# A decoder layer with a top-2 expert stage: gate and residual row move from the last stage into the expert stage

## The chip, the cores and the metric

One core of a Trainium2 chip (trn2) runs the whole layer in one launch. The metric is the device time of that launch in microseconds: the median of three runs. Beside it stands one profiled execution, from which all rows are taken. Names used below: TensorE is PE in the profile, VectorE is DVE, ScalarE is ACT, GpSimd is POOL and SyncE is SP.

## What is computed

Input `x` is 32 sequences of 128 rows of 128 numbers. A first block (an attention block with a scan and a feed-forward part), a cross attention over a context, and an expert layer follow each other, each with a residual and a layer norm. Only the last third matters here:

```python
logits = jnp.einsum('bsh,eh->bse', x, Wr)              # 8 experts
probs = jax.nn.softmax(logits, axis=-1)
top_v, top_i = jax.lax.top_k(probs, 2)
top_v = top_v / jnp.sum(top_v, axis=-1, keepdims=True)  # the two gates
for e in range(8):
    w_e = jnp.sum(jnp.where(top_i == e, top_v, 0.0), axis=-1)
    h = gelu(jnp.einsum('bsh,mh->bsm', x, W1[e]) + b1[e])   # 128 -> 512
    y = jnp.einsum('bsm,hm->bsh', h, W2[e]) + b2[e]         # 512 -> 128
    out = out + y * w_e[..., None]
x = layernorm(x + out)
```

## The kernel before

All is float32. It has a setup, a loop over 8 groups of 4 sequences (tiles of 128 rows), a routing table, an expert stage and a last stage. Five engines run programs of their own, written out by hand, and meet at semaphores; each engine works through its program in order.

**Group loop.** For each group the layer's first two blocks are computed, the router picks two experts per row, and both copies of the row are written to `expert_in` in DRAM by GpSimd (`rows_out`: 8 indirect DMAs, one per sequence and choice). What is written is `xb_rows[k]`, 132 columns wide: 128 of the row and 4 more, of which the first is the row's "home", its place in `expert_out`. VectorE writes the home (L1238) and the normalised row `xb` (`ln_apply`, L1240). ScalarE copies `xb` to the second tile (L652), GpSimd copies it back into `x_all` (L838) for the residual of the last stage. The two gates go to `gate_all` (L1280 to L1283). Later on VectorE computes the slots (`slot_u`, L1302), after which GpSimd may scatter.

**Expert stage.** The rows now lie in `expert_in` ordered by expert, padded to tiles of 128. There are 72 tiles (`TILES`). A table `tab` in SBUF holds each tile's expert and first row; engines read it with `value_load`. For tile j:

- SyncE: `row_in` loads the 128 rows into `xt` (four buffers) once TensorE has turned the tile four before (`turned`); `home_of` loads the four further columns into `home` (eight buffers).
- TensorE: `turn_rows(j+2)`, `hidden(j+1)` (L1773), `outputs(j)` (L1782). `outputs` waits for `y_added` of two tiles before, since it reuses the bank.
- VectorE: `turned_rows(j+2)` copies the turned tile out of its bank (L1349, `xnT`), `weights(j+2)` copies the expert's first matrix (L1355), `results(j)` adds the bias `b2` to the output and writes `ysb` (L1363, `xa`).
- ScalarE: `gelu(j)` (L669).
- GpSimd: `results_out(j)` scatters `ysb` to `expert_out` at the homes (L850).

The tile names are those of the memory that is reused: `xn` is `xt`, `xnT` is `xtT`, `xa` is `ysb`, `qT` is `w1c`, `hT` is `hx`, `mix` is `two_rows`.

**Last stage.** Eight groups again. SyncE loads the two expert results of each row (`rows_back`, L519, 512 KB for a group, four groups in flight). ScalarE multiplies the first by its gate (`first_part`, L685, four instructions), GpSimd adds the residual from `x_all` (`first_sum`, L864), VectorE multiplies the second by its gate and adds (`combine`, L1395, four instructions), then takes statistics (L1401, L1405), GpSimd makes scale and shift of them (`last_scale`, L870 to L880), ScalarE applies them (`last_norm`, L694), SyncE stores (L525). `rows_back(g+4)` is issued behind `store(g)` on SyncE and waits for `combined` of group g.

## Time and profile before

| | us |
|---|---|
| median of 3 runs | 929.15 (928.66 to 929.34) |
| the profiled execution | 929.04 |
| its span, first to last instruction | 927.2 |
| setup and scan, up to the first group's work | about 0 to 100 |
| group loop and routing table, until the first expert tile is loaded | to about 721 |
| expert stage, 72 tiles | about 721 to 881 |
| last stage | 881 to 927.2 |

Busy time over the whole span: TensorE 690.2 us (74%), VectorE 544.1 (59%), ScalarE 373.0 (40%), GpSimd 365.1 (39%). Mean granted clock of TensorE 0.877 of full speed.

How to read the profile: a row gives start, length, engine, line, operation, the tile written and the tiles read, the shape, and in brackets how long the engine had been idle and what ended that. "issue" means that nothing shown in the profile ended the wait: the engine's own sequencer was not there yet. A busy share is an average over stages whose limits differ, so each stage is read by itself.

### The profile page before, as it was taken

How to read it: one execution, taken by the hardware profiler on the slowest of the kernel's cores; microseconds unless marked ns; L12 is line 12 of the kernel's file. 1: busy time of each engine (PE TensorE's matmuls, PEld its weight loads, DVE VectorE, ACT ScalarE, POOL GpSimd, SP SyncE). 2: the span in 40 equal slices, each digit the busy share in tenths (PEclk: the TensorE clock that was granted, in tenths of full speed). 3: DMA queues.
4: the chain of work that ended last, by engine and by line, in shares of the span. 5: the costliest groups of instructions: out<-in, count | busy, mean ns of one | idle time of the engine just before them, and what ended most of it. 6: DMA issues, size and time to landing. Idle time of an engine off the chain costs nothing.

```text
span 927.2 us, 21485 instructions
## 1 busy us (share of the span) xinstructions
PE 690.2 (74%) x6159; PEld 497.4 (54%) x6160; DVE 544.1 (59%) x1733; ACT 373.0 (40%) x790; POOL 365.1 (39%) x514
## 2 busy tenths in 40 slices
PE   4517887896887887886988789788783799999900
PEld 1303645644744753653664564474462799989900
DVE  4585665676666576576576666657656244444443
ACT  2002344353362352443444336235331355555545
POOL 2533260361253145047036026214405255545545
PEclk9557998998997997999899799799797699999955
DMA  8400000000000000000000000000022222222244
GB/s 265 158 12 1 1 31 8 1 20 15 0 12 23 0 12 23 0 12 23 0 0 26 9 0 13 22 0 12 23 90 65 51 63 63 63 61 62 52 150 129
DMA packets 45528, 36.43 MB, mean 39 GB/s; under 512 B 20059, under 2 KB 39452, under 8 KB 45249
## 3 DMA queue, kind: packets, MB, share of 16 engines
q1 hardware_dynamic: 37312, 23.09, 9.0%
q0 software_dynamic: 4608, 9.59, 3.1%
q10 hardware_dynamic: 3584, 3.48, 1.1%
q8 instruction: 9, 0.15, 0.1%
q14 instruction: 15, 0.12, 0.0%
HBM read 23.35 MB, written 12.76 MB: 39 GB/s over the span
## 4 chain that ended last, share of the span: by engine, by line
PE 45%; DVE 19%; issue 11%; another core or an unknown queue 9%; POOL 6%; ACT 3%; DMA 3%; DVEq 1%; SPq 0%; POOLq 0%; ACTq 0%
PE bank L1488 10%; PE bank L1782 8%; PE bank L1773 7%; PE bank L1525 4%; POOL rstd L768 3%; PE bank L1646 3%; DVE stats L1055 3%; PE bank L1573 2%; DVE xn L1064 2%; PE bank L1633 2%; PE bank L1654 2%; PE bank L1615 2%; DVE hT L1104 2%; DVE mv L1060 2%
## 5 line engine op out<-in xcount | busy, mean ns | idle before, releaser
L765 POOL TENSOR_SCALAR vare<-mv 128x1 f32<-128x1 f32 (+1 forms) x112 | 25.9, 231 | 341.1 <-DVE mv L1060 339.5
L850 POOL DMA_INDIRECT expert_out<-xa,home x72 | 80.0, 1111 | 82.6 <-DVE xa L1363 47.7
L669 ACT ACTIVATE hT<-bank,qT 128x128 f32<-128x128 f32 x288 | 81.9, 370 | 64.9 <-PE bank L1773 64.8
L568 ACT ACTIVATE mix<-bank 128x512 f32<-128x512 f32 x128 | 66.1, 602 | 93.8 <-remote 79.0
L1171 DVE TENSOR_REDUCE negmax<-bank 128x4 f32<-128x512 f32 x128 | 79.7, 683 | 18.6 <-remote 10.1
L1782 PE MATMUL bank<-w_t,hT 128*128 x576 | 81.6, 285 | 3.9 <-ACT hT L669 3.9
L799 POOL DMA_INDIRECT expert_in<-xb_rows,slot_u x72 | 71.2, 989 | 25.5 <-issue 19.7
L1773 PE MATMUL bank<-xnT,qT 128*128 128x128 f32 x576 | 80.9, 285 | 0.2
L1104 DVE TENSOR_TENSOR hT<-bank,decay 128x512 f32<-128x512 f32 x72 | 46.4, 686 | 53.6 <-PE bank L1525 53.6
L1488 PE MATMUL bank<-xqT,w_qkv 128*128 128x512 f32 x144 | 71.7, 615 | 5.3 <-DVE x L1160 5.3
L1782 PEld LDWEIGHTS bank<-w_t,hT 128*128 128x128 f32 x576 | 70.8, 194 | 6.3 <-issue 4.9
L1773 PEld LDWEIGHTS bank<-xnT,qT 128*128 128x128 f32 x576 | 72.4, 197 | 3.3 <-issue 2.8
L1488 PE MATMUL bank<-w_qkv,xqT 128*128 128x512 f32 x72 | 52.2, 820 | 29.5 <-ACT mix L568 22.1
L768 POOL TENSOR_TENSOR rstd<-vare,minus_half 128x1 f32<-128x1 f32 (+1 forms) x112 | 67.6, 603 | 9.9 <-POOL vare L765 1.2
L1355 DVE COPY qT<-w_t 128x516 f32 x72 | 31.0, 430 | 43.6 <-issue 39.4
L568 ACT ACTIVATE hebT<-bank 128x512 f32<-128x512 f32 x36 | 21.5, 597 | 86.1 <-PE bank L1573 86.1
L1573 PE MATMUL bank<-hT,v_sb 128*64 128x128 f32 x576 | 39.4, 278 | 15.3 <-DVE x L1160 9.1
L1633 PE MATMUL bank<-qm,kr 32*128 32x128 f32 x512 | 26.8, 335 | 28.5 <-DVE negmax L1171 16.6
L1525 PE MATMUL bank<-qT,kT 64*128 64x128 f32 x576 | 41.8, 285 | 7.3 <-ACT mix L568 5.8
L568 ACT ACTIVATE cT<-bank 128x512 f32<-128x512 f32 x32 | 19.1, 597 | 68.6 <-PE bank L1646 68.6
L1363 DVE TENSOR_TENSOR xa<-bank,b_bc 128x128 f32<-128x128 f32 x72 | 21.0, 292 | 43.7 <-PE bank L1782 29.7
L1633 PEld LDWEIGHTS bank<-qm,kr 32*128 32x128 f32 x512 | 22.4, 235 | 41.7 <-DVE negmax L1171 22.5
(289 smaller groups left out, 1442.9 us busy)
## 6 DMA issues: line engine op xcount, KB each, us to landing
xn<-expert_in SPq DMA_DIRECT2D x72, 64.0 KB
mix<-expert_out SPq DMA_DIRECT2D x8, 512.0 KB, 4.0
ctxT<-in_ctxT SPq DMA_DIRECT2D x9, 256.0 KB, 2.7
w_t<-in_w_t ACTq DMA_DIRECT2D x1, 2064.0 KB, 8.6
xT_all<-in_xT SPq DMA_DIRECT2D x4, 512.0 KB, 5.7
x_all<-in_x SPq DMA_DIRECT2D x4, 512.0 KB, 9.0
w_t<-in_w_t SPq DMA_DIRECT2D x1, 2048.0 KB, 7.4
expert_in<-xb_rows,slot_u POOLq DMA_INDIRECT x72
```

The lines of the kernel that those rows point to most:

```text
L568: nc.scalar.activation(dst, src_ap, func, scale=scale, **kw).then_inc(free[BANK[name]], 1)
L669: ins = nc.scalar.activation(hx[n][:, c, :], bank[2 + n][:, c * P:(c + 1) * P], ACT.Gelu, bias=w1c[n][:, FF + c:FF + c + 1])
L768: nc.gpsimd.tensor_tensor(rstd[stage][:, t:t + n], vare[stage][:, t:t + n], minus_half[:, 0:n], ALU.pow).then_inc(rstd_ready[stage], n)
L799: nc.gpsimd.indirect_dma_start(xs[:, :], bass.IndirectOffsetOnAxis(ap=slot_u[:, t, k:k + 1], axis=0), xb_rows[k][:, t, :], None).then_inc( ...
L850: nc.gpsimd.indirect_dma_start(ys[:, :], bass.IndirectOffsetOnAxis(ap=home[:, n, 0:1].bitcast(U32), axis=0), ysb[n % UNROLL], None).then_i ...
L1104: nc.vector.tensor_tensor(at[t % 2][:, r, :, :], b[:, :].rearrange("p (a n) -> p a n", a=PAIRS), decay[:, t, :].unsqueeze(1).broadcast_to( ...
L1171: nc.vector.tensor_reduce(negmax[t % 2][:, i, 28:28 + XC], b[:, :].rearrange("p (c n) -> p c n", c=XC), AX.X, ALU.max, negate=True).then_i ...
L1488: done(mm(b[:, :], lhsT, rhs, start=True, stop=True), name)
L1525: ins = mm(halves[r][:, tile(p)], kT[rows, p, tile(t)], qT[rows, p, tile(t)], start=True, stop=True)
L1633: ins = mm(b[i][:, tile(c)], kr[rows, c, tile(t)], qm[t % 2][rows, c, :], start=True, stop=True)
L1773: ins = mm(bank[2 + n % 2][:, c * P:(c + 1) * P], w1c[n % 2][:, c * P:(c + 1) * P], xtT[n % 2], start=True, stop=True)
L1782: ins = mm(bank[4 + n % 2][:, 0:P], hx[n % 2][:, c, :], w2_t[:, bass.ds(e, 1), c, :].rearrange("p a n -> p (a n)"), start=(c == 0), stop=( ...
```

## The change

Each scattered row carries what the last stage needed separately. Of the four further columns the first stays the home (`HOME`), the second becomes the row's gate (`GATE`), the third a flag (`OWN`) that is 1 in the copy of the first choice and 0 in the other. VectorE writes the gates straight into `xb_rows`; `gate_all` and GpSimd's copy into `x_all` go. The flag is set once by a memset.

In the expert stage GpSimd multiplies the loaded tile by its flag (`own_rows`, two tiles ahead, into `own`, four buffers), and VectorE's `results` gets a second instruction that multiplies by the gate and adds `own`, after a wait for the first. `y_drained` now tells TensorE that the bank is free; `y_added` comes after the second instruction. SyncE's `row_in` waits also for `own_ready`. VectorE's loop spans eight tiles instead of four.

In the last stage `first_part` and `first_sum` go; VectorE adds the two halves of a group in one instruction. Homes are numbered by partition first, so that the rows of a group that belong to one partition lie together in `expert_out` (4 KB a partition instead of four pieces of 1 KB).

```diff
+HOME, GATE, OWN = P, P + 1, P + 2
...
-        gate_all = sb("gate_all", [P, SEQS, TOPK])
...
-        part = [xf, xab]
+        own = [xab[:, n, :] for n in range(UNROLL)]
...
 # SyncE
             def row_in(j, n, row):
                 sp.wait_ge(turned, j + 1)
+                sp.wait_ge(own_ready, j + 1)
...
-            both = ys[0:SEQS * P * TOPK, :].rearrange("(s p k) n -> p s (k n)", p=P, k=TOPK)
+            both = ys[0:SEQS * P * TOPK, :].rearrange("(p s k) n -> p s (k n)", p=P, k=TOPK)
...
             def rows_back(g, n):
-                sp.wait_ge(combined, g * T + T)
+                sp.wait_ge(combined, g + 1)
...
 # ScalarE: first_part and its calls removed
-                for t in range(T):
-                    ins = nc.scalar.activation(part[n][:, t, :], two_rows[m][:, t, 0, :], ACT.Copy,
-                                               scale=gate_all[:, bass.ds(g * T + t, 1), 0])
...
 # GpSimd
+            nc.gpsimd.memset(xb_rows[0][:, :, OWN:OWN + 1], 1.0).then_inc(pool_const, 1)
...
-                nc.gpsimd.tensor_copy(x_all[:, bass.ds(g * T, T), :], xb[:, :, :]).then_inc(xkept, 1)
...
+            def own_rows(n, xs_in, homes_in):
+                pool.wait_ge(x_in[n % UNROLL], xs_in)
+                pool.wait_ge(home_in[n], homes_in)
+                nc.gpsimd.tensor_scalar(own[n % UNROLL], xt[n % UNROLL], home[:, n, OWN - P:OWN - P + 1], None,
+                                        ALU.mult).then_inc(own_ready, 1)
...
+            with pool.Fori(0, TILES // (2 * UNROLL) - 1) as i:
+                for n in range(2 * UNROLL):
+                    m = n + 2
+                    own_rows(m % (2 * UNROLL), i * 32 + 16 * (m // UNROLL + 1), i * 16 + 16 * (m // (2 * UNROLL) + 1))
                     results_out(i * (2 * UNROLL) + n, n, i * 16 + 16)
...
-                nc.gpsimd.tensor_tensor(acc[m][:, :, :], part[n][:, :, :], x_all[:, bass.ds(g * T, T), :],
-                                        ALU.add).then_inc(sum0_ready, 1)
...
 # VectorE
-                nc.vector.reciprocal(gate_all[:, bass.ds(g * T, T), 0], wsum[:, :])
+                nc.vector.reciprocal(xb_rows[0][:, :, GATE], wsum[:, :])
...
-                nc.vector.tensor_tensor(gate_all[:, bass.ds(g * T, T), 1], ratio[:, :], wrec[:, :], ALU.mult)
+                nc.vector.tensor_tensor(xb_rows[1][:, :, GATE], ratio[:, :], wrec[:, :], ALU.mult)
...
+            def results(j, n, homes_in, ys_out):
+                nc.vector.tensor_tensor(ysb[n % UNROLL], bank[4 + n % 2][:, 0:P],
                                         b2_bc[:, bass.ds(e, 1), :].rearrange("p a n -> p (a n)"), ALU.add
-                                        ).then_inc(y_added, 1)
+                                        ).then_inc(y_drained, 1)
+                dve.wait_ge(own_ready, j + 1 + UNROLL)
+                dve.wait_ge(home_in[n], homes_in)
+                dve.wait_ge(y_drained, j + 1 + 2)
+                nc.vector.scalar_tensor_tensor(
+                    out=ysb[n % UNROLL], in0=ysb[n % UNROLL], scalar=home[:, n, GATE - P:GATE - P + 1],
+                    in1=own[n % UNROLL], op0=ALU.mult, op1=ALU.add).then_inc(y_added, 1)
...
             def combine(g, m, turns):
-                dve.wait_ge(sum0_ready, g + 1 + 2)
-                for t in range(T):
-                    nc.vector.scalar_tensor_tensor(
-                        out=acc[m][:, t, :], in0=two_rows[m][:, t, 1, :],
-                        scalar=gate_all[:, bass.ds(g * T + t, 1), 1],
-                        in1=acc[m][:, t, :], op0=ALU.mult, op1=ALU.add).then_inc(combined, 1)
+                dve.wait_ge(y_back[m], turns)
+                nc.vector.tensor_tensor(acc[m][:, :, :], two_rows[m][:, :, 0, :], two_rows[m][:, :, 1, :], ALU.add
+                                        ).then_inc(combined, 1)
...
 # TensorE, outputs
-                pe.wait_ge(y_added, j + 1)
+                pe.wait_ge(y_drained, j + 1)
```

## Rows read from the trace of the kernel before

**Rows 1.** Busy us by stage: PE, PEld, DVE, ACT, POOL; granted clock, DMA share

```profile
783.00:823.00 40.00, 39.96 (x332) 38.45 (x331) 18.36 (x58) 21.73 (x76) 21.54 (x20) 1.00 0.25 61
692.00:700.00 8.00, 5.74 (x61) 4.91 (x61) 5.88 (x27) 1.19 (x2) 3.90 (x10) 1.00 0.00 0
```

**Rows 2.** Chain of waits from 690 us: shares by line, then start, us, what

```profile
by line: PE bank L1782 29.3%; PE bank L1773 28.2%; issue 7.5%; DMA mix<-expert_out 5.0%; PE bank L1766 3.6%; POOL expert_in L799 2.7%; ACT xb_rows L694 1.8%; ACT L669 1.6%; ACT hT L669 1.4%; POOL rstdc L873 1.3%; DMA expert_in<-xb_rows,slot
...
883.51 3.88 DMA mix<-expert_out
```

**Rows 3.** Line L1359, VectorE sequencer: duration ns min/median/max, first and last start

```profile
L1359 DVEq TENSOR_LOAD <-tab x67: 298/303/319, 735.2 to 873.8; - x67
```

**Rows 4.** Instructions in order of time, VectorE and GpSimd, expert stage

```profile
768.13 0.43 DVE L1355 COPY qT<-w_t 128x516 f32 x1 [0.56 <-issue]
...
768.96 0.29 DVE L1363 TENSOR_TENSOR xa<-bank,b_bc 128x128 f32<-128x128 f32 x1 [0.40 <-issue]
769.17 0.28 DVE L1349 COPY xnT<-bank 128x128 f32<-128x128 f32 x1
...
770.00 0.43 DVE L1355 COPY qT<-w_t 128x516 f32 x1 [0.55 <-issue]
770.07 1.19 POOL L850 DMA_INDIRECT expert_out<-xa,home  x1 [0.68 <-issue]
...
770.93 0.29 DVE L1363 TENSOR_TENSOR xa<-bank,b_bc 128x128 f32<-128x128 f32 x1 [0.50 <-issue]
...
771.41 0.29 DVE L1349 COPY xnT<-bank 128x128 f32<-128x128 f32 x1 [0.19 <-issue]
```

**Rows 5.** Line L1363, whole run, and what ended its idle time: us, times

```profile
L1363 DVE TENSOR_TENSOR xa<-bank,b_bc x72: 291/292/293, 731.0 to 879.9; 128x128 f32<-128x128 f32 x72
...
  PE bank L1782: 29.7, 47
```

**Rows 6.** Instructions in order of time, GpSimd and VectorE, group loop

```profile
627.22 0.61 POOL L838 COPY x_all<-xb_rows 128x512 f32 x1
...
627.33 0.58 DVE L1064 TENSOR_SCALAR xn<-xheb,mv,rstd 128x128 f32<-128x128 f32 x1
...
628.10 0.57 POOL L768 TENSOR_TENSOR rstd<-vare,minus_half 128x1 f32<-128x1 f32 x1
...
629.99 0.34 DVE L1064 TENSOR_SCALAR xn<-xheb,mv,rstd 128x128 f32<-128x128 f32 x1
```

**Rows 7.** Line L1395, first group of the last stage: duration ns min/median/max

```profile
L1395 DVE SCALAR_TENSOR_TENSOR x<-mix,gate_all,x x4: 340/350/1355, 890.5 to 892.3; 128x128 f32<-128x128 f32 x4
```

**Rows 8.** Order of time: a dependent pair on VectorE; GpSimd beside L1395

```profile
683.26 0.26 DVE L1185 RECIPROCAL rsum<-bank 128x16 f32<-128x16 f32 x1 [1.43 <-PE bank L1654]
683.55 0.29 DVE L1187 TENSOR_TENSOR cx<-bank,rsum 128x128 f32<-128x128 f32 x1
...
890.87 1.33 POOL L864 TENSOR_TENSOR x1b<-xab,x_all 128x512 f32<-128x512 f32 x1 [0.59 <-ACT xab L685]
```

**Rows 9.** GpSimd, lines L736 and L850: duration ns min/median/max

```profile
L736 POOL TENSOR_SCALAR lnb_cols<-ones,ln_b x1: 703/703/703, 36.1 to 36.1; 128x128 f32<-128x128 f32 x1
...
L850 POOL DMA_INDIRECT expert_out<-xa,home x72: 956/1191/1207, 732.2 to 881.0; - x72
```

**Rows 10.** Page, part 5, costliest groups: busy us, mean ns, idle before

```profile
L1104 DVE TENSOR_TENSOR hT<-bank,decay 128x512 f32<-128x512 f32 x72 | 46.4, 686 | 53.6 <-PE bank L1525 53.6
```

**Rows 11.** Instructions in order of time, last stage

```profile
889.02 1.31 ACT L685 ACTIVATE xab<-mix,gate_all 128x128 f32<-128x128 f32 x4 [0.22 <-DMA mix<-expert_out]
...
892.53 0.86 DVE L1401 BATCH_NORM_STATS2 stats<-x 128x6 f32<-128x128 f32 x4
...
893.95 0.34 POOL L870 TENSOR_SCALAR varec<-mvc 128x4 f32<-128x4 f32 x1 [1.75 <-DVE mvc L1405]
...
896.18 1.65 ACT L694 ACTIVATE x<-x,shiftc,rstdc 128x128 f32<-128x128 f32 x4 [4.38 <-POOL shiftc L880]
...
922.78 0.37 SPq L525 DMA_DIRECT2D out<-xb_rows  x1
```

More of the change, by code:

```diff
@@ L348, in bass_decoder @@
             sem("dve_held"), sem("pool_held"), sem("sp_held"), sem("act_held"))
-        part_ready, sum0_ready = sem("part_ready"), sem("sum0_ready")
+        own_ready, y_drained = sem("own_ready"), sem("y_drained")
         LN3, LN2, LNA, LNB = range(4)
@@ L696, in last_norm @@
                 ins.then_inc(outc_ready, 1)
-            first_part(0, 0, 16)
-            first_part(1, 1, 16)
-            with act.Fori(0, G // 4 - 1) as i:
+            with act.Fori(0, G // 4) as i:
                 for m in range(4):
-                    first_part(i * 4 + (m + 2), (m + 2) % 4, i * 16 + (16 + 16 * ((m + 2) // 4)))
                     last_norm(i * 4 + m, m, i * 32 + (16 * (m // 2) + 1))
-            for g in range(G - 4, G):
-                if g + 2 < G:
-                    first_part(g + 2, (g + 2) % 4, 16 * (G // 4))
-                last_norm(g, g % 4, 16 * (g // 2) + 1)
         @block.gpsimd
@@ L881, in last_scale @@
                                         ).then_inc(rstdc_ready, 1)
-            pool.sem_inc(sum0_ready, 2)
             pool.sem_inc(outc_ready, 4)
-            first_sum(0, 0)
-            with pool.Fori(0, G // 4 - 1) as i:
+            with pool.Fori(0, G // 4) as i:
                 for m in range(4):
-                    first_sum(i * 4 + (m + 1), (m + 1) % 4)
                     last_scale(i * 4 + m, m)
-            for g in range(G - 4, G):
-                if g + 1 < G:
-                    first_sum(g + 1, (g + 1) % 4)
-                last_scale(g, g % 4)
         @block.vector
@@ L1375, in _ @@
                 weights(n + 2, n % 2)
-                results(n, None, n)
-            with dve.Fori(0, TILES // UNROLL - 2) as i:
-                for n in range(UNROLL):
-                    turned_rows(i * UNROLL + (UNROLL + n + 2), n % 2)
-                    weights(i * UNROLL + (UNROLL + n + 2), n % 2)
-                    results(i * UNROLL + (UNROLL + n), i, n)
+                results(n, n, 16, None)
+            with dve.Fori(0, TILES // (2 * UNROLL) - 1) as i:
+                for n in range(2 * UNROLL):
+                    m = n + UNROLL
+                    turned_rows(i * (2 * UNROLL) + (m + 2), n % 2)
+                    weights(i * (2 * UNROLL) + (m + 2), n % 2)
+                    results(i * (2 * UNROLL) + m, m % (2 * UNROLL), i * 16 + 16 * (m // (2 * UNROLL) + 1),
+                            i * 32 + 16 * (m // UNROLL))
             for n in range(UNROLL):
```

57 lines of the change are left out of this document (26 added, 31 removed).

## The prediction

> **What bounds the kernel now.** I read busy time by stage first, then the chain of waits, then the single instructions of the stage that the change loads. The kernel has three parts that matter here: the loop over 8 groups, the expert stage of 72 tiles (about 721 to 881 us), and the last stage (881 to 927 us).
>
> In the expert stage TensorE is busy in 39.96 of 40 us at a granted clock of 1.00, VectorE in 18.36 [rows 1]. The chain from 690 us on gives the two expert matmul lines 29.3% and 28.2% [rows 2]. So TensorE looks like the bound and VectorE looks half idle. The second is misleading. VectorE's instructions are short, but between them its sequencer reads an expert number out of a tile (`value_load`) twice per tile, 303 ns each time [rows 3], and then does register work. The rows of VectorE show what that makes of a tile [rows 4]: from `xa` (`results`) to the next `xnT` copy 0.21 us (768.96 to 769.17), from there to the weight copy 0.83 (770.00), from a weight copy to the next `xa` 0.83 (768.13 to 768.96) or 0.93 (770.00 to 770.93), and the idle time before these last two is put down to "issue", not to TensorE. At the loop's branch, once in four tiles, `xa` to `xnT` is 0.48 instead of 0.21 (770.93 to 771.41). With the smaller step four tiles take 4 x (0.21 + 0.83 + 0.83) + 0.27 = 7.75 us, with the larger 8.15. So VectorE's own cycle is 1.94 to 2.04 us a tile; I take 2.00. The stage runs at (879.9 - 731.0) / 71 = 2.097 us a tile [rows 5]. TensorE and VectorE are both nearly saturated; what VectorE gets beyond 0.1 us a tile is paid.
>
> In the last stage nothing is saturated; a long chain through all engines sets the pace.
>
> **Part 1, the group loop.** GpSimd loses one copy of 0.61 us per group (L838). What GpSimd makes right behind it (628.10 plus 0.57) is used by VectorE only at 629.99, so the copy's own time is covered. But beside it VectorE's `xn` took 0.58 us at 627.33, against 0.34 at 629.99 for the same form [rows 6], and VectorE works without a pause there. Eight groups x 0.2 = 1.6 us gained (0 to 2). The gates are written to another tile by the same two instructions: nothing. The added memset of one column lies in the loading phase: nothing, 0.1 at most.
>
> **Part 2, VectorE in the expert stage.** Each `results` gets one `scalar_tensor_tensor` of 128x128 that depends on the addition in front of it. Its own length is 340 to 350 ns where it isn't held [rows 7]. What counts is the step: the dependent instruction can start when the addition has finished, 0.29 us plus the way through the semaphore; the pair `rsum`, `cx` with a wait of the same kind starts 0.29 apart at a duration of 0.26, so 0.03 [rows 8]. That makes 0.32 to 0.33; the other two new waits (`own_ready`, `home_in`) fit in that time, and their tiles were served long before. After it the `turned_rows` copy follows at the 0.21 it has now, since the sequencer goes on while the instruction runs. Two more thresholds that depend on the loop's counter: 0.03 (0 to 0.1). The loop now spans eight tiles, so the branch's 0.27 is paid half as often: -0.03. Cycle: 2.00 + 0.33 + 0.03 - 0.03 = 2.33; bounds 2.24 (1.94 + 0.30) and 2.45. Queued behind the longer `results` on VectorE are `turned_rows` and `weights` of the tile three ahead, and TensorE waits for both; they are late by just that much. TensorE then idles about 0.3 us a tile; that the clock stays up under this I take from 692 to 700 us, where it is 1.00 with TensorE busy 5.74 of 8 us [rows 1].
>
> **Part 3, GpSimd in the expert stage.** Each tile gets a `tensor_scalar` of 128x128 with a scalar from a tile. Same form: 0.70 us (L736) [rows 9]. Its other work is the scatter: it starts 0.82 us after `xa` has ended (768.96 + 0.29 to 770.07), takes 1.19 there, where VectorE's weight copy had begun before it (770.00) [rows 4], and 0.96 at the least [rows 9]. New cycle: order is `own_rows` two tiles ahead, then wait for `y_added`, then scatter. 0.82 + 1.15 + 0.1 to get the next instruction out = 2.07, and the 0.70 lies in the 0.82 of the next tile. GpSimd fits a cycle of 2.33, but barely. Where it matters is when it reads: counted from the start of one `scalar_tensor_tensor`, the scatter ends at 0.35 + 0.82 + 1.15 = 2.32 and `own_rows` starts at about 2.42, while VectorE's next `scalar_tensor_tensor` starts at about 2.30 in seven of eight tiles and at 2.7 behind the branch. What an overlap costs in the wrong order is in the trace: one of four such VectorE instructions took 1355 ns instead of 350 while GpSimd's addition of 1.33 us ran [rows 7, 8]. So behind the branch VectorE is held to 2.42 + 0.70 = 3.1, 0.4 us in one of eight tiles, 0.05 a tile; 0.02 for weight copies held now and then. Cycle 2.40 us.
> The Trainium skill, SBUF — State Buffer, section "Who interferes with whom", says that a VectorE instruction with two SBUF inputs contends with a GpSimd instruction that reads SBUF, and that whichever issues first keeps the shared pair for its whole length. The held row agrees with it. By that rule alone, without the order of starts, each tile could pay; that is the second rival.
>
> **Part 4, SyncE.** `row_in` also waits for `own_ready`, and `home_of` of the same tile and all later loads are queued behind it. `own_rows` of a tile ends about 3 us after TensorE has turned that tile; the load it holds back is needed four tiles (9.6 us) after the turning. Even at the 3.88 us that a load of eight times its size takes [rows 2] it is covered by over 2 us. If GpSimd fell behind by two tiles, that cover would be gone and TensorE would wait for rows.
>
> **Part 5, the last stage.** Removed per group: four ScalarE copies, one GpSimd addition of 128x512, four `scalar_tensor_tensor`. Added: one VectorE addition of 128x512 with both inputs in SBUF; nearest row the 128x512 addition with one of them in a bank, 686 ns [rows 10]. VectorE per group: 0.69 + 0.1, then statistics and aggregation, from 892.53 to 0.2 before GpSimd's start at 893.95, 1.2, with gaps 2.2 us. GpSimd per group: from 893.95 until ScalarE starts at 896.18, 2.2 us with the hop. ScalarE 1.65 [rows 11]. Counting from the first landing (883.51 + 3.88 = 887.39 [rows 2]): the first group is through VectorE at 2.3, GpSimd at 4.7, ScalarE at 6.4; then its store and the fifth load are issued (7.0), and that load lands at 11.0. The first four groups have left VectorE at 9.0, so it waits 2.0 us; four more groups end at 11.1 + 4 x 2.2 = 19.9, GpSimd at 22.2, ScalarE at 24.0, last store at 24.2. Now the last store starts at 922.78 - 887.39 = 35.4 [rows 11]. Gain 11.2 us; bounds 9 (2.4 us a group and a slower fifth load) and 13 (loads land sooner).
> The homes numbered by partition make each partition's piece of a load 4 KB instead of four of 1 KB; I count nothing for it, and the bound of 13 holds what it may bring. The Trainium skill, DMA: Bandwidth & Descriptors, section "Specifications", names 512 B as the least transfer for line rate. By that rule both sizes are beyond it and the term is nothing, as in the sum.
> The last tile's way to its scatter grows by 0.35 us.
>
> **The sum.** Against the profiled execution (929.04 us, span 927.2; the median of the runs is 929.15, 0.1 off): 929.04 - 1.6 + 0.35 - 11.2 - 148.9 + 71 x T = 767.7 + 71 x T. With T = 2.40 this is 938.1 us.
>
> **The rivals.**
> *A, the forecast.* VectorE's cycle becomes the bound: T between 2.30 and 2.55, 931 to 949 us. For it: the "issue"-ended waits.
> *B, GpSimd's read comes first.* If `own_rows` starts before the `scalar_tensor_tensor` in ordinary tiles too, it holds it each time: T = 2.42 + 0.6 = 3.0, 981 us; in half of the tiles 960. Against it: about 0.1 us of lead for VectorE by the sum above, which is no more than its error.
> *C, the extra instruction is hidden (faster).* If the sequencer's reads turn out to run beside the new instruction and its wait, T stays at 2.10, and the last stage's gain is kept: 916.8 us. It decides from T below 2.27. For it: VectorE is busy in only 46% of the stage, and 47 of 72 `xa` waited for TensorE [rows 5]. Against it: the wait for the addition stands in the sequencer itself, so nothing behind it can begin.
> *D, the last stage gains next to nothing.* If the loads with their new order take the stage over (four in flight, the fifth behind a store), the 11 us are missing: 949 us. Against it: with four loads in flight the second kept ScalarE waiting for only 0.22 us (889.02) [rows 11]. This is also the case in which the change doesn't do what it says.
>
> **How the numbers follow.** A 0.55, B 0.17, C 0.18, D 0.10. Predicted 938.1. The range leaves out the lower half of C and the upper half of B: 922 to 964. 0.2% of this kernel is 1.9 us, about what a measurement can tell from no change. Faster (below 927.3): most of C, 0.14. Same: the edge between C and A, 0.05. Slower: 0.81.
>
> **What the profile of the changed kernel would show.** Expert stage: (last `xa` - first `xa`) / 71 near 2.40; TensorE with idle time before the hidden matmul, put down to VectorE; `xa` to `scalar_tensor_tensor` 0.33 apart; lengths of the latter near 0.35 in most tiles, near 1 in one of eight (A) or in most (B). Group loop: the four `xn` all near 0.34. Last stage: stores 2.2 us apart but for one gap of 4; last store some 24 us behind the first landing. The prediction is wrong if TensorE's pace stays 2.1, if the granted clock falls in the expert stage, or if GpSimd and not VectorE sets the cycle.

## The result, and the profile after

| | us |
|---|---|
| kernel before, median of 4 runs beside those of the changed one | 929.25 (928.66 to 931.14) |
| changed kernel, median of 4 runs | 936.49 (934.92 to 936.90) |
| ratio | 1.0071, 95% interval 1.0053 to 1.0090 |
| the profiled execution of the changed kernel | 934.92, span 933.1 |

The change makes the kernel 0.7% slower; 938.1 us was predicted, in a range of 922 to 964. The profiled execution is the shortest of the four, so the account below adds up to 5.9 us, not to the 7.2 between the medians. It goes by two rows in each kernel: the first and the last result tile `xa` of the expert stage (731.0 and 879.9 before [rows 5], 727.1 and 894.8 after).

| | before | after | difference | predicted |
|---|---|---|---|---|
| until the first `xa` | 731.0 | 727.1 | -3.9 | -1.6 |
| first to last `xa` (71 tiles) | 148.9 | 167.7 | +18.8 | +21.5 |
| a tile | 2.097 | 2.362 | +0.265 | 2.40 |
| last `xa` to the end of the span | 47.3 | 38.3 | -9.0 | -10.85 |

The expert stage, in windows of busy time (the columns of [rows 1]):

```profile
783.00:823.00 40.00, 37.85 (x289) 34.03 (x289) 21.66 (x67) 18.94 (x67) 30.55 (x34) 1.00 0.22 55
```

TensorE, which was busy in 39.96 of these 40 us, has 37.85 left, at the same granted clock; VectorE went from 18.36 to 21.66 and GpSimd from 21.54 to 30.55. The line of the result tile, and what ended the idle time before it (us, times), the answer to [rows 5]:

```profile
L1348 DVE TENSOR_TENSOR xa<-bank,b_bc x72: 288/292/293, 727.1 to 894.8; 128x128 f32<-128x128 f32 x72
...
  issue: 25.1, 58
  PE bank L1774: 7.1, 13
```

Before, 47 of 72 results waited for TensorE; now 13 do, and 58 come when VectorE's own sequencer gets to them. This split alone is weak evidence: the changed kernel's second profile, at the end of the experiments, has the same tile (2.356 us) and puts 40 results down to TensorE and 31 to "issue". The order of time says more. VectorE's instructions, the answer to [rows 4]:

```profile
786.67 0.29 DVE L1348 TENSOR_TENSOR xa<-bank,b_bc 128x128 f32<-128x128 f32 x1 [0.34 <-issue]
787.10 0.37 DVE L1354 SCALAR_TENSOR_TENSOR xa<-xa,home,xab 128x128 f32<-128x128 f32 x1
...
788.15 0.43 DVE L1340 COPY qT<-w_t 128x516 f32 x1 [0.48 <-issue]
...
788.97 0.29 DVE L1348 TENSOR_TENSOR xa<-bank,b_bc 128x128 f32<-128x128 f32 x1 [0.40 <-PE bank L1774]
789.40 0.35 DVE L1354 SCALAR_TENSOR_TENSOR xa<-xa,home,xab 128x128 f32<-128x128 f32 x1
789.67 0.28 DVE L1334 COPY xnT<-bank 128x128 f32<-128x128 f32 x1
790.42 0.43 DVE L1340 COPY qT<-w_t 128x516 f32 x1 [0.47 <-issue]
791.25 0.29 DVE L1348 TENSOR_TENSOR xa<-bank,b_bc 128x128 f32<-128x128 f32 x1 [0.40 <-issue]
```

The last of these tiles takes 0.43 + 0.27 + 0.75 + 0.83 = 2.28 us from one `xa` to the next; of the 71 steps 54 lie between 2.27 and 2.38 us. Of the 0.43 in front of the new instruction (`scalar_tensor_tensor`, STT from here on) 0.29 are the addition itself; 0.14 pass until the STT that depends on it starts. TensorE's hidden and output matmuls beside these rows, then a run of output matmuls of the kernel before:

```profile
788.68 1.13 PE L1765 MATMUL bank<-xnT,qT 128*128 128x128 f32 x8
789.65 1.15 PE L1774 MATMUL bank<-w_t,hT 128*128 x8
```

```profile
767.66 1.15 PE L1782 MATMUL bank<-w_t,hT 128*128 x8
```

The hidden matmuls start 0.10 us behind the end of the weight copy (788.58), and 62 of 70 weight copies are followed by them within 0.13 us; in the kernel before it is 16 of 70. The output matmuls end at 790.80, 0.45 us before the next result starts (791.25), and 0.45 is also the median of the 72. In the kernel before they end at 768.81 and the result starts 0.15 us later [rows 4]; 40 of its 72 results start within 0.16 us of that end, in the changed kernel 4 of 72. TensorE now waits for VectorE, and VectorE no longer for TensorE: the bound has passed from one engine to the other. GpSimd beside VectorE's rows, in order of time, and the whole line of the STT (ns min/median/max):

```profile
786.94 0.61 POOL L841 TENSOR_SCALAR xab<-xn,home 128x128 f32<-128x128 f32 x1
788.29 1.18 POOL L832 DMA_INDIRECT expert_out<-xa,home  x1 [0.73 <-issue]
789.51 0.71 POOL L841 TENSOR_SCALAR xab<-xn,home 128x128 f32<-128x128 f32 x1
```

```profile
L1354 DVE SCALAR_TENSOR_TENSOR xa<-xa,home,xab x72: 350/351/505, 727.5 to 895.2; 128x128 f32<-128x128 f32 x72
```

GpSimd's `own_rows` began first at 786.94, the STT at 787.10 while it ran, and took 0.37 us. No STT of the 72 was held for the length of `own_rows`, which was what rival B needed. Of the 72 scatters 68 start 0.82 to 0.84 us behind the end of their STT: GpSimd waits for VectorE, and not the other way round.

The group loop, by the last instruction of the routing in two neighbouring groups, kernel before and then after:

```profile
557.48 0.17 DVE L1302 CAST slot_u<-slot_f 128x8 uint32<-128x8 f32 x1
...
632.58 0.17 DVE L1302 CAST slot_u<-slot_f 128x8 uint32<-128x8 f32 x1
```

```profile
258.69 0.17 DVE L1286 CAST slot_u<-slot_f 128x8 uint32<-128x8 f32 x1
...
333.46 0.17 DVE L1286 CAST slot_u<-slot_f 128x8 uint32<-128x8 f32 x1
```

75.10 us a group before, 74.77 after. In these groups TensorE's granted clock is at its lower level for a part of the time (0.91 in the mean); there are shorter ones of 73.3 to 73.9 us with a mean clock of 0.93, one of the seven intervals before and three after.

The last stage, VectorE's first instruction of groups 1, 2 and 5 to 8, and SyncE's queue:

```profile
902.79 0.69 DVE L1388 TENSOR_TENSOR x<-mix 128x512 f32<-128x512 f32 x1 [7.22 <-DMA mix<-expert_out]
...
904.96 0.69 DVE L1388 TENSOR_TENSOR x1b<-mix 128x512 f32<-128x512 f32 x1
...
913.73 0.69 DVE L1388 TENSOR_TENSOR x<-mix 128x512 f32<-128x512 f32 x1 [1.99 <-DMA mix<-expert_out]
...
916.89 0.69 DVE L1388 TENSOR_TENSOR x1b<-mix 128x512 f32<-128x512 f32 x1 [1.05 <-DMA mix<-expert_out]
...
919.98 0.69 DVE L1388 TENSOR_TENSOR xbk<-mix 128x512 f32<-128x512 f32 x1 [0.89 <-ACT x L685]
...
922.14 0.69 DVE L1388 TENSOR_TENSOR cumg<-mix 128x512 f32<-128x512 f32 x1
```

```profile
898.86 1.76 SPq L520 DMA_DIRECT2D mix<-expert_out  x4
909.45 0.34 SPq L526 DMA_DIRECT2D out<-x  x1
909.91 0.36 SPq L520 DMA_DIRECT2D mix<-expert_out  x1
...
928.64 0.38 SPq L526 DMA_DIRECT2D out<-xb_rows  x1
```

The first group is summed from 902.79 on, the last store starts 25.9 us later, 26.1 us behind the landing of the first load; before it was 35.4 behind that landing [rows 2, 11].

### The profile page after: what moved, and what is told of

Read it like the earlier page. It is cut to its first block, busy times and chain, and to the rows that moved or that the text cites. A ratio compares the mean times of both kernels' runs of the same rounds, so it can differ in the third digit from the quotient of the medians.

```text
span 933.1 us, 21706 instructions
## 1 busy us (share of the span) xinstructions
PE 700.7 (75%) x6159; PEld 497.8 (53%) x6160; DVE 564.6 (61%) x1781; ACT 362.8 (39%) x758; POOL 401.9 (43%) x571
## 4 chain that ended last, share of the span: by engine, by line
PE 41%; DVE 21%; issue 13%; another core or an unknown queue 8%; POOL 5%; ACT 3%; DVEq 3%; DMA 2%; SPq 1%; ACTq 0%; POOLq 0%
PE bank L1480 9%; PE bank L1765 6%; PE bank L1774 5%; PE bank L1517 4%; POOL rstd L753 3%; PE bank L1638 3%; DVE stats L1039 3%; PE bank L1625 2%; PE bank L1565 2%; DVE xn L1048 2%; PE bank L1607 2%; ACT mix L569 2%; DVE hT L1088 2%; PE bank L1646 2%
## 5 line engine op out<-in xcount | busy, mean ns | idle before, releaser
L569 ACT ACTIVATE hebT<-bank 128x512 f32<-128x512 f32 x36 | 21.5, 597 | 86.1 <-PE bank L1565 86.1
L841 POOL TENSOR_SCALAR xab<-xn,home 128x128 f32<-128x128 f32 x72 | 49.4, 687 | 10.0 <-DMA home<-expert_in 6.8
```

The costliest lines, as they stand in the source:

```text
L569: nc.scalar.activation(dst, src_ap, func, scale=scale, **kw).then_inc(free[BANK[name]], 1)
```

## The experiments

All twelve ran beside the kernel before. The chips differ, by the rows, in one thing: on those of the first two sets (before: 929 and 930 us) TensorE's clock was at its lower level for a part of every group; on those of the other two (before: 874 and 875 us) it was 0.96 or more in every group of the changed kernel. The page's row of the granted clock, changed kernel, first and last set:

```profile
PEclk9557997997997997998999899799795999999975
```

```profile
PEclk9556999999999999999999999999987999999965
```

So each kernel is read against before in its own set, and across sets only by the expert stage, where the clock is 1.00 behind the first tiles (0.72 in the 5 us around the first `xa` of the kernel before) and the changed kernel's tile took 2.362 and 2.356 us.

| kernel | us, median | ratio to before (95%) | `xa`, first to last | a tile |
|---|---|---|---|---|
| no STT on VectorE | 912.36 | 0.980 (0.977 to 0.984) | 727.1 to 874.8 | 2.08 |
| no `own_rows`, four row buffers | 958.20 | 1.031 (1.029 to 1.034) | 726.6 to 918.1 | 2.70 |
| expert number kept | 927.19 | 0.997 (0.996 to 0.999) | 724.2 to 886.5 | 2.29 |
| no `own_rows`, number kept | 956.51 | 1.029 (1.027 to 1.032) | 723.1 to 914.4 | 2.69 |
| no `own_rows`, eight row buffers | 885.12 | 1.012 (1.009 to 1.015) | 678.2 to 847.1 | 2.38 |
| the same, number kept | 879.15 | 1.005 (1.004 to 1.007) | 675.6 to 839.7 | 2.31 |
| old numbering of homes | 883.49 | 1.011 (1.009 to 1.013) | 674.2 to 842.2 | 2.37 |
| copy put back | 886.65 | 1.014 (1.012 to 1.016) | 680.4 to 847.6 | 2.36 |
| STT moved | 874.66 | 0.9995 (0.998 to 1.001) | 674.3 to 832.5 | 2.23 |
| STT moved, number kept | 872.68 | 0.997 (0.995 to 0.9985) | 674.6 to 830.6 | 2.20 |
| `own_rows` with two arrays | 883.21 | 1.0085 (1.0065 to 1.0105) | 677.0 to 845.6 | 2.38 |
| changed kernel again | 882.74 | 1.0091 (1.0070 to 1.0112) | 673.9 to 841.2 | 2.36 |

The theory is that VectorE's cycle, longer by one dependent instruction, is the bound (V). The rival is GpSimd's cycle (G): by rows of the changed kernel `own_rows` 0.71, a gap of 0.35, the scatter 1.18 and 0.05 more also come to 2.29 us.

**No STT on VectorE.** GpSimd keeps all it has; gate and row are not applied.

```diff
             def results(j, n, homes_in, ys_out):
                 nc.vector.tensor_tensor(ysb[n % UNROLL], bank[4 + n % 2][:, 0:P], ...
-                                        ).then_inc(y_drained, 1)
-                dve.wait_ge(own_ready, j + 1 + UNROLL)
-                dve.wait_ge(home_in[n], homes_in)
-                dve.wait_ge(y_drained, j + 1 + 2)
-                nc.vector.scalar_tensor_tensor(out=ysb[n % UNROLL], ...).then_inc(y_added, 1)
+                                        ).then_inc(y_added, 1)
```

> The changed kernel without the second VectorE instruction of each result (its output lacks the gate and the residual row: that part of the computation is left out); GpSimd still makes own_rows. Theory V (VectorE's own cycle sets the expert stage's 2.36 us a tile): the cycle falls to TensorE's, 2.10, total about 918 us. Theory G (GpSimd sets it: 0.71 for own_rows, 0.35 to the scatter, 1.18 for the scatter, 0.05, together 2.29): the stage stays at 2.29 or more, total 931 or more.

The tile is 2.08 us again. The same window of busy time, and what ended the idle time before the result:

```profile
783.00:823.00 40.00, 39.93 (x329) 38.04 (x328) 18.14 (x58) 21.86 (x77) 32.32 (x38) 1.00 0.26 63
```

```profile
  PE bank L1768: 33.8, 58
```

TensorE is full again with 39.93 of 40 us, 58 of 72 results wait for it, and GpSimd, with all its new work, keeps a cycle of 2.08. G is out as the cause; the STT, with its waits, costs the 0.28 us a tile.

**No `own_rows` on GpSimd.** The STT adds the row where it landed; the gates are doubled and EPS multiplied by four, so the output is the same.

```diff
-                nc.gpsimd.tensor_scalar(own[n % UNROLL], xt[n % UNROLL], ...).then_inc(own_ready, 1)
...
-                    in1=own[n % UNROLL], op0=ALU.mult, op1=ALU.add).then_inc(y_added, 1)
+                    in1=xt[n % UNROLL], op0=ALU.mult, op1=ALU.add).then_inc(y_added, 1)
...
             def row_in(j, n, row):
-                sp.wait_ge(own_ready, j + 1)
+                sp.wait_ge(y_added, j + 1)
```

> The changed kernel without own_rows on GpSimd. VectorE's second instruction adds the loaded row itself in both copies, the gates are doubled and the last norm's epsilon is four times as large, so that the sum is twice the old one and its norm is the same. VectorE does what it did. Theory V: 2.36 us a tile as before (2.30 to 2.40), total 932 to 937. Theory G: 2.10, total 918.

Neither: 958 us, 2.70 us a tile. The waits of the whole run (engine, line, what it waited for: us, times, longest) and the window:

```profile
PE bank L1740 <- DMA xn<-expert_in: 43.5, 39, 17.3
```

```profile
783.00:823.00 40.00, 33.41 (x245) 29.46 (x244) 19.60 (x60) 17.76 (x59) 15.86 (x15) 1.00 0.20 50
```

With one instruction less in the stage TensorE is busy in only 33.41 of 40 us, and it waits for rows. `own_rows` does more than multiply: it empties the landing buffer early. Without it each of the four buffers is held until its tile's result is finished, and the next load into it starts too late. The edit made a new bound and so tells nothing of V and G.

**Expert number kept.** For six of eight tiles `results` uses the number that `weights` of that tile read two tiles earlier; the second register load goes.

```diff
             def weights(j, n):
                 e = dve.value_load(tab[0:1, 0, bass.ds(j, 1)], min_val=0, max_val=EXP - 1)
                 ...
+                return e
-            def results(j, n, homes_in, ys_out):
-                e = dve.value_load(...)
+            def results(j, n, homes_in, ys_out, e=None):
+                if e is None:
+                    e = dve.value_load(...)
```

> The changed kernel; in the loop over eight tiles VectorE reads the expert's number once a tile and keeps it in a register for the result two tiles later (six of eight tiles). All data instructions stay. That takes some 0.5 us of sequencer work from six of eight VectorE cycles. Theory V alone: VectorE falls to about 1.95 and TensorE's pace of 2.10 is left, total 918. Theory G: GpSimd's 2.29 stays, total 931. If both cycles are equally long, as their rows suggest, the result is G's.

2.29 us a tile and 927.19 us, 0.3% under the kernel before. A load costs 0.30 us [rows 3], but six loads in eight tiles brought 0.075 us a tile. Something near 2.29 takes over, and G's sum is exactly that number. The runs without `own_rows`, further on, show that the agreement was chance.

**No `own_rows` and number kept.** Both edits together.

> Both edits together: no own_rows on GpSimd, expert number read once. Neither theory leaves a bound above TensorE's own: 2.07 to 2.10 us a tile, total 915 to 918 us, below the kernel before. If it stays above 925, something else bounds the stage, such as the way from the last matmul through the two dependent VectorE instructions.

2.69 us: the late rows cover everything, and this pair too was left open.

**No `own_rows`, eight row buffers.** The buffers of `own` are free in this version; with them the rows have eight, and a load can go out eight tiles ahead. TensorE's loop is written over eight tiles for it.

```diff
-        xt = [xn[:, n, :] for n in range(UNROLL)]
+        xt = [xn[:, n, :] for n in range(UNROLL)] + [xab[:, n, :] for n in range(UNROLL)]
...
-            dve.sem_inc(y_added, UNROLL)
+            dve.sem_inc(y_added, 2 * UNROLL)
```

> The multiplication own_rows is gone from GpSimd as in the run before it without it (the STT on VectorE adds the row where it landed, gates are doubled and EPS is multiplied by four, so the result is the same), but the rows now have eight buffers instead of four, so a load can be eight tiles ahead. If the load that came too late was what cost that run 0.34 us a tile, TensorE's waits for rows disappear and the bound falls back to VectorE's own cycle, which has not changed by an instruction: 2.36 us a tile, 934 to 938 us. If GpSimd's cycle (own_rows 0.71 + gap 0.35 + scatter 1.18 + 0.05 = 2.29 us) or its writes beside VectorE's work set the pace after all, the tile falls to 2.10 to 2.25 us and the time to 915 to 928. If the slow run had another cause than late rows, it stays near 2.70 us and 955 to 960.

From 2.70 to 2.38 us a tile: the late rows were the cause of that run's loss, and with them gone the tile is back at the changed kernel's, though GpSimd has 0.7 us of work less in each. That is V, and it settles G once more: GpSimd's reads beside VectorE's and its cycle cost nothing here.

**The same, number kept.**

> As the version with eight row buffers and no own_rows, and the expert's number is read once for six of eight tiles and kept in a register until the results need it. GpSimd's chain by its rows is then the scatter's 1.2 us alone, and VectorE's loses most of one register load (0.30 us and what stands around it) in six of eight tiles. Theory VectorE-then-GpSimd (with the number kept GpSimd's 2.29 us was the next bound): both are gone, and the tile falls to TensorE's full rate, 2.08 to 2.12 us, so 914 to 920 us: under the kernel before by 1.0 to 1.6 per cent. If VectorE's cycle itself stood at 2.29 us in the kept version, nothing comes of taking own_rows away: 2.27 to 2.30 us, 926 to 930 us.

2.31 us, where 2.08 to 2.12 was expected. GpSimd now idles 98 us before its scatters and the tile is no shorter than with `own_rows` (2.29). So the 2.29 was not GpSimd's. What it is, two engines show together; VectorE and then TensorE in order of time:

```profile
767.14 0.29 DVE L1332 TENSOR_TENSOR xa<-bank,b_bc 128x128 f32<-128x128 f32 x1 [0.61 <-PE bank L1759]
...
768.59 0.43 DVE L1322 COPY qT<-w_t 128x516 f32 x1 [0.48 <-issue]
...
771.43 0.28 DVE L1332 TENSOR_TENSOR xa<-bank,b_bc 128x128 f32<-128x128 f32 x1
```

```profile
769.23 1.06 PE L1750 MATMUL bank<-xnT,qT 128*128 128x128 f32 x8
770.12 1.12 PE L1759 MATMUL bank<-w_t,hT 128*128 x8
```

A result at 767.14 is followed by its STT, the transposed copy and the weight copy, which ends at 769.02. The hidden matmuls that need these weights start at 769.23, the output matmuls queued behind them end at 771.24, and the result two tiles on starts at 771.43: 4.29 us for two tiles, 2.15 for one, plus the tiles that still read their number. This loop passes through both engines, neither of which is full. The STT lies in it with 0.42 us for two tiles. In the changed kernel it was not yet the bound: the output matmuls ended 0.45 us before the result there, against 0.15 where the result follows them at once, so it had about 0.3 us to spare in two tiles. With the number kept that is used up: 44 of 72 results start within 0.16 us of the end of their output matmuls in that run, and 33 in this one, against 4 in the changed kernel. This is why six loads of 0.30 us brought so little.

**STT moved.** The STT of a tile comes after the next transposed copy and the next weight copy, ahead of the next result.

```diff
-                nc.vector.scalar_tensor_tensor(...).then_inc(y_added, 1)
+            def added(j, n, homes_in):
+                dve.wait_ge(own_ready, j + 1 + UNROLL)
+                dve.wait_ge(home_in[n], homes_in)
+                dve.wait_ge(y_drained, j + 1 + 2)
+                nc.vector.scalar_tensor_tensor(...).then_inc(y_added, 1)
...
                     turned_rows(m + 2, n % 2)
                     weights(m + 2, n % 2)
+                    added(m - 1, ...)
                     results(m, ...)
```

> The changed kernel with one instruction moved on VectorE: the STT that applies gate and row for a tile comes after the next transposed copy and the next weight copy, just ahead of the next result, instead of right behind its own. Nothing else changes. In the changed kernel the pieces of a normal tile are 0.43 (result to STT, of which 0.12 is waiting for the result's own signal), 0.27, 0.76 and 0.83 us, together 2.29. Theory (VectorE's own cycle is the bound, and the signal it waits for is part of it): the 0.12 us goes, the rest stays, 2.17 us for a normal tile and about 2.25 for the mean, so 71 x 0.11 = 8 us less than the changed kernel in the same call: about its ratio to before minus 0.8 per cent. Rival (GpSimd's chain own_rows - scatter of 2.29 us paces as well): the mean stays at 2.33 to 2.37 us and the time within 2 us of the changed kernel's.

2.23 us a tile and 874.66 us, 8.1 less than the changed kernel in the same set, as expected: from 1.009 of the kernel before to 0.9995. The same instructions in another order win back what the change had lost. Behind its result the STT had to wait for the signal; ahead of the next result it lies where VectorE was idle for 0.40 us until its sequencer got there, and it is out of the way of the two copies. Median tile: 2.16 us. The order brings a new cost, though. VectorE and GpSimd, in order of time:

```profile
749.85 0.43 DVE L1340 COPY qT<-w_t 128x516 f32 x1 [0.54 <-issue]
750.19 0.46 DVE L1356 SCALAR_TENSOR_TENSOR xa<-xa,home,xab 128x128 f32<-128x128 f32 x1
...
752.00 0.85 DVE L1340 COPY qT<-w_t 128x516 f32 x1 [0.60 <-issue]
```

```profile
749.73 1.03 POOL L832 DMA_INDIRECT expert_out<-xa,home  x1 [0.73 <-issue]
...
751.60 1.02 POOL L832 DMA_INDIRECT expert_out<-xa,home  x1 [0.18 <-issue]
```

The weight copy at 749.85 starts 0.12 us into a scatter and takes 0.43; the one at 752.00 starts 0.40 us into the next and takes 0.85, until 0.23 us behind the scatter's end. In the changed kernel the line's median is 430 ns, here it is 500.

**STT moved and number kept.**

> The moved STT, and the expert's number kept in a register for six of eight tiles; own_rows stays on GpSimd with its four row buffers. The kept number alone gave 2.287 us a tile. If the bound there was GpSimd's chain (0.71 + 0.35 + 1.18 + 0.05 = 2.29 us), this gives 2.27 to 2.30 again. If it was the loop result - STT - transposed copy - weight copy (1.88 us) - TensorE's two times eight matmuls (2.2 us) for two tiles, which the run with eight buffers and the kept number points to (2.31 us there with no own_rows at all), the STT has left that loop and the tile falls to TensorE's full rate or near it, 2.08 to 2.16 us: 13 to 20 us less than the changed kernel, 6 to 12 us less than the kernel before.

2.20 us a tile, 872.68 us: the lowest of all versions in that set, 0.3% under the kernel before and 1.1% under the changed one. 2.27 to 2.30 would have spoken for GpSimd's chain, which is complete in this version; with the STT out of the loop the tile falls below it. It does not reach the 2.08 to 2.16 of the loop theory either. The held weight copies, whose mean rises from 446 to 601 ns (700 to 830 us of both runs), are of the right size for that; no run here took them away alone. Nor did any run give the kernel before its number kept, so how much of the 0.3% belongs to the change isn't shown.

**Old numbering of homes.** Loads of the last stage in 1 KB pieces, all else as changed.

```diff
-            both = ys[0:SEQS * P * TOPK, :].rearrange("(p s k) n -> p s (k n)", p=P, k=TOPK)
+            both = ys[0:SEQS * P * TOPK, :].rearrange("(s p k) n -> p s (k n)", p=P, k=TOPK)
```

> The changed kernel with the homes numbered as before the change (sequence, partition, half), so that the last stage's loads are made of 1 KB pieces instead of 4 KB ones. The prediction says 0: four groups are in flight, and the median landing was 4.0 us with the small pieces in the kernel before and is 4.6 us with the large ones. Then 935 to 938 us. If the numbering by partition does shorten the loads, those that end late now (the fifth group's sum waits 2.0 us for its data, the sixth's 1.1 us) end later still, by 1 to 3 us a group on the way of the last store: 939 to 946 us. If the large pieces are what makes the fifth load late, 932 to 934.

883.49 us at a ratio of 1.0109 (1.0086 to 1.0133), beside the changed kernel's 882.74 at 1.0091 (1.0070 to 1.0112) in another set: no difference that these intervals show. The traces have a small one. From the issue of the first loads to the last store are 30.5 us here (846.33 to 876.80) and 29.5 (845.23 to 874.72) and 29.8 in two executions with the new numbering. So the large pieces are worth 0.7 to 1.0 us at most.
The Trainium skill, DMA: Bandwidth & Descriptors, section "Specifications", names 512 B as the least transfer for line rate, by which both sizes should be alike; within 1 us of a stage of 30 they are.

**Copy put back.** The 128x512 copy on GpSimd again at its place in the group loop.

```diff
                 ln_scale(LN3, g + 1, 2)
+                nc.gpsimd.tensor_copy(x_all[:, bass.ds(g * T, T), :], xb[:, :, :]).then_inc(xkept, 1)
                 ln_scale(LN3, g + 1, 3)
```

> The changed kernel with GpSimd's copy of the normalised rows (into the array that nobody reads now) put back into the group loop, at its place before the last scaling. The prediction has its removal at -0.2 us a group and 1.6 in all; the profile of the changed kernel shows 74.79 us for a group against 75.10 before, 0.31 a group and 2.5 us in eight. Theory: the copy held the following scaling and with it the slots; put back, the group is 75.1 again and the time 1.6 to 2.5 us longer, 937.5 to 939.5 us. Rival: what was gained in the first 730 us is TensorE's clock in that one execution alone (three groups of 73.3 to 73.9 us), and the copy hides: 936.0 to 937.0 us and a group of 74.8.

The copy and VectorE's `xn` beside it, then a short group of this run and a short group of the changed kernel on a chip of the same kind:

```profile
583.29 0.61 POOL L823 COPY x_all<-xb_rows 128x512 f32 x1
```

```profile
583.41 0.58 DVE L1051 TENSOR_SCALAR xn<-xheb,mv,rstd 128x128 f32<-128x128 f32 x1
```

```profile
315.71 0.17 DVE L1289 CAST slot_u<-slot_f 128x8 uint32<-128x8 f32 x1
...
383.46 0.17 DVE L1289 CAST slot_u<-slot_f 128x8 uint32<-128x8 f32 x1
```

```profile
583.44 0.17 DVE L1286 CAST slot_u<-slot_f 128x8 uint32<-128x8 f32 x1
...
650.91 0.17 DVE L1286 CAST slot_u<-slot_f 128x8 uint32<-128x8 f32 x1
```

67.75 against 67.47 us, both with a mean clock of 1.00; among the groups with 0.98 it is 68.66 here and 68.35 in the version with eight buffers, which has no copy. So the copy costs 0.28 to 0.31 us a group, and `xn` is held to 0.58 us again. The changed kernel's own longer groups, at 0.96 to 0.97, took 67.96 to 68.19 us, though, which would make it 0.5: the size is less sure than the sign. The time of 886.65 us is 4 us above the changed kernel's (ratios 1.0137 and 1.0091), more than the 2.2 us of eight groups; the whole loop differs by 3.8 us between executions without the copy (473.6 to 477.5 us from the first to the last slot list), so the time alone could not have sized it.

**`own_rows` with two arrays.** The row times its flag, the flag read as a second array of 128 columns.

```diff
-                nc.gpsimd.tensor_scalar(own[n % UNROLL], xt[n % UNROLL], home[:, n, OWN - P:OWN - P + 1], None, ...
+                nc.gpsimd.tensor_tensor(own[n % UNROLL], xt[n % UNROLL],
+                                        home[:, n, OWN - P:OWN - P + 1].broadcast_to([P, P]), ...
```

> The changed kernel with own_rows written as a multiplication of two arrays (the row and its flag, broadcast over the 128 columns) instead of an array by one scalar of each partition; same values. The prediction's rival B rested on the row in which an STT beside GpSimd's two-array addition took 1355 ns instead of 340, but the changed kernel never showed one held (350/351/505 ns over 72). If it is the second array that GpSimd reads which holds the STT, some of the 72 STTs that start beside own_rows now take 0.6 to 0.9 us, own_rows itself is longer, and the mean tile rises to 2.5 to 2.9 us: 10 to 38 us more than the changed kernel. If the held row had another cause (its 128x512 size, or what ran beside it), the STT stays at 0.35 us and the time within 3 us.

The lines of the STT and of `own_rows`, then one pair in order of time, VectorE and GpSimd:

```profile
L1355 DVE SCALAR_TENSOR_TENSOR xa<-xa,home,xab x72: 350/352/558, 677.4 to 846.1; 128x128 f32<-128x128 f32 x72
```

```profile
L841 POOL TENSOR_TENSOR xab<-xn,home x72: 393/512/529, 671.3 to 842.7; 128x128 f32<-128x128 f32 x72
```

```profile
785.74 0.55 DVE L1355 SCALAR_TENSOR_TENSOR xa<-xa,home,xab 128x128 f32<-128x128 f32 x1
```

```profile
785.71 0.42 POOL L841 TENSOR_TENSOR xab<-xn,home 128x128 f32<-128x128 f32 x1
```

Nine STTs that began 0.01 to 0.05 us into such an `own_rows` took 0.52 to 0.56 us, until 0.16 us behind its end. So there is a hold, but only for as long as GpSimd's instruction runs, and this form runs 0.41 us; the tile stays at 2.38. The expected 0.6 to 0.9 us supposed an `own_rows` longer than the one-scalar form's 0.61 us; it is shorter.

**Changed kernel again.**

> The changed kernel unaltered, as the measure for the other three of this call and for its own ratio to before on this chip: 1.0071 by the first measurement. The two earlier versions that leave its expert stage as it is (old numbering; copy put back) gave 1.0109 and 1.0137 on a chip whose TensorE clock is not halved in the group loop. Theory: the stage's loss (18.8 us) and the gains elsewhere are in microseconds and do not depend on the clock, so the ratio is 1.007 to 1.010 on either kind of chip. Rival: the first ratio was helped by TensorE's clock and the true one is 1.010 to 1.013.

1.0091 (1.0070 to 1.0112) on a chip whose clock stays up, beside 1.0071 (1.0053 to 1.0090) on the first. The intervals overlap: the loss holds on both kinds of chip, and whether the first ratio was helped a little by the clock stays open.

## Why the prediction was right

**The bound.** Right, and shown: taking the STT away gives 2.08 us, as before (2.10), taking GpSimd's new work away gives nothing. The sign that it named came under another name: TensorE's idle time before the hidden matmul is there, but the profile puts 7.0 us of it down to "issue" and none to VectorE; only the order of time shows that it follows the weight copy. VectorE looked 46% busy, but the steps between its instructions left only 0.1 us in a tile.

**The size of VectorE's step.** The mean tile was predicted at 2.40 us and took 2.36. Errors of both signs met. With the steps read one by one the prediction's normal tile comes to 0.33 + 0.21 + 0.83 + 0.83 = 2.20 us; it took 2.28, and 2.31 in the median. The term "0.32 to 0.33" for the dependent pair was too small: 0.43 in the rows above, since the way through the signal took 0.14 us here and 0.03 in the pair that it was read from [rows 8]. And the following copy came 0.27 after the STT, not 0.21. On the other side the weight copy came 0.75 behind that copy, not 0.83, and 0.07 us were put in for holds ("0.05 held behind the branch, 0.02 for weight copies"), and `own_rows` held no STT for more than 0.04 us. At a branch the tile is longer by 0.5 us (2.83), once in eight tiles, where the sum had 0.27; with three tiles of 2.61 to 2.71 and some short ones at both ends the mean is 2.36. That it came within 0.04 of the prediction is partly luck.

**Rival B.** Wrong by its mechanism, not by its order of starts: `own_rows` was running when the STT began in 18 of the 72 tiles. The row of 1355 ns [rows 7] was made beside a GpSimd addition of two 128x512 arrays and 1.33 us [rows 8]; that row was carried over to a multiplication of half the length with one array and a scalar.

**Rival C.** Hidden work: no. The one extra dependent instruction costs 0.28 us a tile against the run without it; it runs for 0.35.

**Group loop.** Direction and mechanism right, the size not: 0.28 to 0.33 us a group instead of 0.2. The held `xn` alone accounts for 0.24 of it. The other 1.5 us before the first `xa` go with the three short groups of the profiled execution, in which TensorE's clock was higher; that the change has no part in that isn't shown.

**Last stage.** Mostly right: 9.0 us where 10.85 were predicted. Up to the fifth group the sum held to 0.2 us: its addition came 10.9 us after the first one (11.1 predicted). The failed step is "four more groups end at 11.1 + 4 x 2.2". From the fifth to the eighth addition 8.4 us passed instead of 6.6: the sixth waited 1.05 us for its load, the seventh started 3.1 us after the sixth. By the landings in the trace all four additions start 0.22 to 0.23 us behind the landing of their load, the seventh too, whose wait the profile puts down to ScalarE. The sixth's load was issued 2.8 us after the fifth's, behind a store, and the four took 3.6, 4.0, 4.9 and 4.8 us from issue to landing. So the later groups hang on the store in front of their load and on the load, not on VectorE's 2.2 us: this is rival D's mechanism, at a price of some 2 us and not of 11.

**Layout.** Counted as nothing; it is worth 0.7 to 1.0 us in the traces and nothing that the times show.

**What was not seen ahead.** The order. The change puts the dependent instruction right behind its source, where VectorE waits for it; and it lies there in a loop result - STT - copies - matmuls, closed every two tiles, which takes over as soon as VectorE's cycle gets shorter by some 0.15 us. Moved by two instructions it costs 8 us less, and with the number kept as well the kernel gets 0.3% below the one before.

## What to carry to other kernels

Read an engine's cycle from start to start of its instructions, waits of its sequencer and register loads included; a busy share of half can mean a full engine. Here the instruction that depends on the one in front of it paid its source's whole length and a signal as well (0.29 + 0.14 us): put independent work between two such instructions. The name that a profile gives to the end of a wait can change from one execution to the next at the same pace; the distance from the other engine's last instruction did not (0.45 us in both profiles of the changed kernel). An instruction that only copies or scales may be what frees a buffer early; before taking it out, ask who waits for that buffer next.

## What the runs showed of the hardware

The way through a signal on one engine was mostly 0.13 to 0.14 us for the STT behind the addition, against 0.03 for a dependent pair elsewhere in the same kernel [rows 8]; why they differ stays open.

A VectorE copy of 128x516 in SBUF is held by GpSimd's scatter, but not by every part of it: in the version with the STT moved, copies that started up to 0.3 us into a scatter took 0.43 us, and nearly all that started 0.35 to 0.65 us into it ran until 0.22 to 0.31 us behind its end (0.61 to 0.90 us). It isn't a fixed phase of every scatter: in the kernel before two copies that started 0.43 and 0.45 us into one of 1.0 us took 0.43. The other order costs GpSimd: in the changed kernel the 46 scatters that started 0.10 to 0.15 us behind a weight copy took 1.17 to 1.22 us, the 8 whose copy began 0.20 to 0.30 us into them 1.02 to 1.03.
The Trainium skill, SBUF — State Buffer, section "Who interferes with whom", says that such copies can take the ports that VectorE shares with GpSimd, and that whoever issues first blocks the other for its whole instruction. The held copies and the longer scatters agree with it; the copies that started within the first 0.3 us of a scatter, and were not held, do not fit "whole instruction".

An STT with two inputs in SBUF that started 0.14 to 0.59 us into GpSimd's one-scalar multiplication took 0.35 to 0.39 us, with no hold of that multiplication's 0.61 (lengths on GpSimd are rough in the profile); beside the two-array form, started within its first 0.05 us, it took 0.52 to 0.56.
The same section of the Trainium skill says that a VectorE instruction with two SBUF inputs contends with a GpSimd instruction that reads SBUF. Here the two-array form bears it out and the one-scalar form hardly does: the STT lost at most 0.04 us beside it.
